# Writing the one-hot comparisons of a graph layer's edge stage as three-operand instructions

## The reference, cut to what matters

```
x_src = node_embeddings[src];  x_dst = node_embeddings[dst];  e = edge_emb[edge_type]
messages = (x_src + e) @ msg_W + msg_b
att_in = concatenate([x_src, x_dst, e, task_rep], axis=-1)
edge_delta = tanh(_gelu(att_in @ att_W1 + att_b1) @ att_W2 + att_b2)
edge_weight = 1.0 + edge_scale * edge_delta
messages = messages * edge_weight
agg = segment_sum(messages, dst, num_segments=n_nodes)
deg = segment_sum(edge_weight[:, 0], dst, num_segments=n_nodes)
```

## Time and profile before

| | us |
|---|---|
| median of 3 runs | 1439.61 |
| the three runs | 1430.62, 1439.61, 1441.83 |
| profiled execution | 1435.78 |
| its span in the trace | 1433.9 |
| POOL, DVE, PE busy in the span | 960.2, 901.2, 920.2 |

### The profile page before, as it was taken

One profiled execution on the slowest core, in us unless ns is written; L12 is line 12 of the kernel. 1 busy time (PEld: TensorE's weight loads), 2 busy tenths in 40 slices (PEclk: granted clock), 3 DMA queues, 4 the chain that ended last, 5 costly groups with the idle time before them and its releaser, 6 DMA issues. The chain is left out here.

```text
span 1433.9 us, 18420 instructions
## 1 busy us (share of the span) xinstructions
PE 920.2 (64%) x4908; PEld 710.1 (50%) x4908; DVE 901.2 (63%) x2653; ACT 614.9 (43%) x1493; POOL 960.2 (67%) x906
## 2 busy tenths in 40 slices
PE   5503232321135110488879999999899999998795
PEld 4402122221125100376767776767677777766464
DVE  5466575656566544146547887777777777876357
ACT  5424333333334333122245665555555555654334
POOL 3477777777777776485566777777777777776012
PEclk9856566665555555698999999999999999999788
DMA  5477566566856565237355777777777777778402
GB/s 149 121 194 273 194 199 220 202 207 201 304 195 215 195 215 199 53 97 181 96 167 172 217 219 216 212 208 218 215 212 217 216 218 222 216 211 176 107 16 75
DMA packets 105090, 266.56 MB, mean 186 GB/s; under 512 B 25067, under 2 KB 45680, under 8 KB 98848
## 3 DMA queue, kind: packets, MB, share of 16 engines
q0 software_dynamic: 54560, 166.61, 39.8%
q1 hardware_dynamic: 48640, 97.03, 21.3%
q10 hardware_dynamic: 1792, 1.75, 0.4%
HBM read 195.82 MB, written 68.81 MB: 185 GB/s over the span
## 5 line engine op out<-in xcount | busy, mean ns | idle before, releaser
L670 POOL DMA_INDIRECT gath<-hp_d,chain_src x391 | 387.0, 990 | 131.4 <-issue 121.0
L1333 POOL DMA_INDIRECT gbuf<-pm_d,srcs x357 | 384.1, 1076 | 123.3 <-issue 104.2
L904 DVE SCALAR_TENSOR_TENSOR hist<-hist,smask,gath 128x256 f32<-128x256 f32 x390 | 189.1, 485 | 207.6 <-ACT gath L700 199.5
L700 ACT ACTIVATE gath<-gath,chain_w 128x256 f32<-128x256 f32 x391 | 167.4, 496 | 336.6 <-DMA gath<-hp_d,chain_src 336.6
L1440 PE MATMUL ps<-qw,halves 128*128 x1275 | 212.5, 275 | 41.3 <-DMA gbuf<-pm_d,srcs 23.8
L1646 DVE TENSOR_TENSOR acc<-ps,acc 112x272 f32 x425 | 186.9, 440 | 77.1 <-DVE acc L1646 47.4
L1442 PE MATMUL ps<-gbuf,ident 128*128 128x256 f32 x714 | 214.3, 382 | 0.0
L822 PE MATMUL ps<-win_hot,node_hot 128*112 128x28 bf16 x391 | 42.3, 246 | 234.2 <-DVE win_hot L1003 234.2
L1514 ACT ACTIVATE gbuf<-ps 128x512 f32<-128x512 f32 x180 | 107.5, 598 | 193.0 <-PE ps L1442 192.7
L1440 PEld LDWEIGHTS ps<-qw,halves 128*128 128x128 bf16 x1275 | 125.1, 98 | 124.1 <-issue 59.7
L1461 PE MATMUL ps<-gbuf,placed 128*112 128x272 f32 x714 | 179.0, 393 | 1.0 <-ACT placed L1535 1.0
(11 more groups left out here) (277 smaller groups left out, 1398.9 us busy)
## 6 DMA issues: line engine op xcount, KB each, us to landing
hist_d<-hist SPq DMA_DIRECT2D x48, 1024.0 KB, 4.5
pm_d<-gbuf SPq DMA_DIRECT2D x7, 896.0 KB, 5.5
gath<-hp_d,chain_src POOLq DMA_INDIRECT x391, 3.0
wn<-node_row_d SPq DMA_DIRECT2D x27, 224.0 KB, 3.5
key<-node_row_d SPq DMA_DIRECT2D x26, 224.0 KB, 3.3
gbuf<-pm_d,srcs POOLq DMA_INDIRECT x357, 4.0
hp_d<-hpo SPq DMA_DIRECT2D x7, 448.0 KB, 3.2
hb_d<-gbuf SPq DMA_DIRECT2D x7, 448.0 KB, 3.4
```

The source lines that it names most:

```text
L670: eng.indirect_dma_start(row_at(j), None, hp_d[:, :], bass.IndirectOffsetOnAxis(ap=chain_src[:, j:j + 1], axis=0)).then_inc(got[q % RINGG] ...
L700: eng.activation(row_at(j), row_at(j), ACT.Copy, scale=chain_w[:, j:j + 1]).then_inc(gw_ready, 1)
L904: eng.scalar_tensor_tensor(out=state_at(j), in0=state_at(j - 1) if j else first_state[:, :], scalar=smask[:, j:j + 1], in1=row_at(j), op0= ...
L1333: eng.indirect_dma_start(gath3(g % RING)[:, k, 0:2 * D], None, pm_d[:, :], bass.IndirectOffsetOnAxis(ap=srcs[:, g * SG + k:g * SG + k + 1] ...
```

## The change

Three comparisons of the edge stage are written as `scalar_tensor_tensor`, which computes (in0 op0 scalar) op1 in1. `hot`: the keys are compared with `pcol` as before, and the result is multiplied by `onec`, read 512 times over. Types and places: 0.0 is added to the index, and the result is compared with the edge's number. The values written are the same. DVE waits once more, for `one_set`, ahead of the stage. No instruction is added, dropped or moved on any engine; three change their kind.

```
 def match_keys(g):
     n, at = g // KG, g % KG * GW
     eng.wait_ge(key_in[n % 2], (n // 2 + 1) * 32)
-    eng.tensor_scalar(hot[g % 2], key[n % 2][:, at:at + GW], pcol[:, 0:1], None, ALU.is_equal).then_inc(hot_ready, 1)
+    eng.scalar_tensor_tensor(out=hot[g % 2], in0=key[n % 2][:, at:at + GW], scalar=pcol[:, 0:1],
+                             in1=onec.to_broadcast([P, GW]), op0=ALU.is_equal, op1=ALU.mult).then_inc(hot_ready, 1)
+eng.wait_ge(one_set, 1)
 match_keys(0)
...
     if has(g):
         e0 = g * (2 * SG)
-        eng.tensor_tensor(gath3(r)[:, :, 2 * D:SW], bc(iof[:, 0:TY], SG), bi(edgef[:, e0:e0 + SG], TY), ALU.is_equal)
-        eng.tensor_tensor(place[r % 3][:, :].rearrange("p (k t) -> p k t", k=SG), bc(iof[:, 0:WIN], SG),
-                          bi(edgef[:, e0 + SG:e0 + 2 * SG], WIN), ALU.is_equal).then_inc(match_ready, 1)
+        eng.scalar_tensor_tensor(out=gath3(r)[:, :, 2 * D:SW], in0=bc(iof[:, 0:TY], SG), scalar=0.0,
+                                 in1=bi(edgef[:, e0:e0 + SG], TY), op0=ALU.add, op1=ALU.is_equal)
+        eng.scalar_tensor_tensor(out=place[r % 3][:, :].rearrange("p (k t) -> p k t", k=SG), in0=bc(iof[:, 0:WIN], SG),
+                                 scalar=0.0, in1=bi(edgef[:, e0 + SG:e0 + 2 * SG], WIN),
+                                 op0=ALU.add, op1=ALU.is_equal).then_inc(match_ready, 1)
```

## The result

The changed kernel took 1420.14 us, the median of 4 runs (1415.54 to 1424.87); the kernel before, run beside it on the same chip, 1435.11 us (4 runs, 1429.71 to 1441.83). The ratio is 0.9882, with a 95% interval of 0.9851 to 0.9913: 1.2% faster, 17 us by this ratio (the two medians differ by 15.0 us), where the forecast was 30 us and 1406 us. The profiled execution took 1415.54 us with a span of 1413.5 us, 20.4 us less than the profiled span before.

A forecast was written before the change was run, and what follows sets the result against it. POOL's gathers were taken to bound the edge stage at 5.47 us a group; falling to 5.16, between PE's 5.10 and VectorE's 5.23, over 97 groups saves 30 us from 1436: 1406 us, range 1393 to 1434.

The forecast's parts named there:

- GpSimd sets the pace: Edge stage: four gathers with 0.30 us ahead of each take 5.50 us, against 5.47 us a group measured.
- L1636, 0.35 us of VectorE, costs POOL half a microsecond: Edge stage, short key comparison: once a group a gather takes about 1.44 us where 0.95 is undisturbed.
- the even-spread formula: Gathers starting evenly: a VectorE instruction of length L holds them (L - 0.17)^2 / 2 / 1.25 us a group.
- end less 0.12: A gather starting inside a VectorE instruction with two SBUF inputs is released 0.12 us before that instruction's end.
- the locking: Edge stage: gathers fall in step with VectorE's 5.03 us period, the last held only 0.03 us by the new key comparison.
- I take 5.16: Edge stage's expected us a group, between PE's floor 5.10 and VectorE's 5.23; from 5.47 now, 30 us gained.
- VectorE's catching up: Edge stage: VectorE, 0.15 us over PE's 4.88 in ordinary steps, recovers in the 14 long ones, 1.4 us to spare.
- VectorE's lag doesn't reach PE: Edge stage: PE waiting for `halves` or `placed` would show VectorE's longer step reaching PE and the forecast wrong.
- the second, holds spread evenly: Edge stage: evenly spread holds, or the new instruction at its upper bound, 5.32 to 5.44 us a group; chance 0.17.
- No hold (the first): Edge stage: by the skill's rule no gather is held, 5.10 us a group, 1394 to 1400 us; chance 0.12.
- Running on into the next instruction (the third): Edge stage: the key comparison's hold continues into the first L1659, 5.49 us a group, 1438 us; chance 0.10.
- The fourth: Edge stage: places, key comparison and L1659 hold as one 1.51 us block, 5.93 us a group, 1481 us; chance 0.08.

The follow-up runs named there:

- the padded runs: The kernel before, short key comparison kept, an unused sum over 256 columns (0.41 us) put behind it; three runs: 1558.88, 1571.24, 1576.85 us, ratios 1.0017, 0.9934, 1.0017.

## Why the prediction came out right, and where it failed

- **GpSimd sets the pace: right.** The gathers' mean fell by 0.053 us, four a group over 97 groups make 21 us, and the stage became 20 us shorter. On the chips where GpSimd waits for PE instead, shorter gathers moved the time by nothing that repeated.
- **"L1636, 0.35 us of VectorE, costs POOL half a microsecond": this step failed.** The gather of the earlier trace rows is held by L1650, which starts 0.01 us before it, and with L1650 left out such a gather takes 0.94 to 0.99 us. Of 0.50 us a group, 0.33 stand at the types and places, 0.14 at the keys, 0.05 elsewhere (rounded). Even of the 0.14 only about 0.05 is L1636's own, if it lets a gather go 0.13 us before its end as in the padded runs; the other 0.09 is L1659's behind it. The half microsecond a group put on L1636 was about 0.05. The row of L1650 stood beside the gather in the very group that I cited; I took the instruction that started inside the gather, and priced L1650 at 0.08 us by the even-spread formula. What should have warned me: the same arithmetic that the prediction used for L904, end less 0.12, fits L1650 to 0.01 us and says nothing of L1636 there.
- **The gain came nevertheless, by the locking** that the prediction had as its second argument: with a step of about 5.03 us four gathers fit one step and fall into the same place each time. It named the wrong place (0.60 us into the key comparison; it is 0.03), but the period was right, 5.03 us predicted and measured. That the range held rests on this and on the measured size of the holds, 0.50 us a group, which stayed right whichever instruction made them; it was luck that writing L1636 longer removes holds of another instruction.
- **"I take 5.16": mis-sized, 5.27 measured.** The gain was 20 us in the profiled executions, not 30, and the forecast proper, 5.10 to 5.23 us a group and 1400 to 1412 us, was missed; the mean gather is 1.023 us, not 0.96 to 1.01. That VectorE's catching up would bring the stage close to PE's pace left out the holds that remain. Of them 0.14 us a group stand at the places, 0.11 at the keys and about 0.06 elsewhere. VectorE's step is 5.5 to 5.6 us at each long group of PE (6.39 us), which breaks the lock, and in most cases a gather meets the place comparison right after it; and 12 of the 63 gathers that start inside the key comparison are held by up to 0.92 us.
- **The three-operand key comparison: right,** 748 ns against 0.75; **types and places cost nothing: right,** 215 and 617 ns.
- **VectorE's lag doesn't reach PE: right.** PE's ordinary groups are 4.88 us and its long ones about 6.4, as before, and VectorE's waits for GELU fell from 40.8 + 15.8 us to 16.9 + 1.1. "Busy about 43 us more" came out as 30.4 in the page: the key comparison did add 80.0 - 37.1 = 42.9, but the custom instructions behind it became 8 us shorter; the rest I didn't trace.
- **The rivals.** The nearest in pace is the second, holds spread evenly: 5.32 us a group predicted, 5.27 measured, although the holds aren't spread evenly at all. No hold (the first) is refuted by 801.57. Running on into the next instruction (the third) happens: that gather, started 0.03 us into the key comparison, ends at 803.43, 0.95 us after 802.48, and the key comparison ended at 802.28, so it was held into the custom instruction behind it. Under the new form it happens 12 times in 101 groups. In the kernel before it was the usual course, 25 of the 31 gathers that started inside L1636, as the prediction saw at 780.45 and gave to this rival alone, not to its own account of the half microsecond. And a start within the first 0.05 us doesn't escape by itself: 24 of those 25 started 0.04 or 0.05 us into L1636. The fourth, a block from the place comparison through to the custom instruction, is refuted: gathers held by the place comparison are let go before it ends, under the long key comparison as under the short.

## What to carry to other kernels

When two engines disturb each other, look at every instruction that overlaps the one that is held, and fit the moment of release to the end of each; the one that starts in its middle is only one candidate, and a count over all gathers sorted by their start can tell them apart without a run. Where a periodic step of one engine meets a periodic queue of another, a step as long as the queue's can be worth more than a shorter one: 0.4 us of added VectorE work a group shortened the gathers, and the kernel with it became faster. And such a gain lasts only where that queue sets the pace: on another chip the same kernel gained nothing that could be told.

## What the runs showed of the hardware

- A place comparison with two SBUF inputs, 0.62 us, holds a gather that starts within its first 0.45 us, until 0.12 us before its end, and then the gather takes its full 0.95 us (1.42 to 1.46 us for a start at its beginning).
- A gather that starts 0.17 to 0.24 us before the types comparison, 0.21 us with two SBUF inputs, is caught by it (1.24 us at 903.54); with the place comparison behind, it takes up to 1.80 us (1.78 at 1196.17). Gathers 0.32 us or more ahead of the types comparison, 0.45 ahead of the places, aren't held. Why one that already runs for 0.2 us is held and starts over, no run here shows.
- The Trainium skill, "SBUF — State Buffer", "Who interferes with whom", says that an instruction with two SBUF inputs contends with what GpSimd reads, and infers that it leaves the writing of descriptors alone. For these gathers the measurement decides otherwise: 1.43 us with it, 0.94 to 0.99 without. The gathers read their row numbers from SBUF (`srcs`); whether that is the reason, no run here shows.
- The short key comparison and a gather hold each other. A gather that starts 0.03 to 0.06 us into it takes 1.10 to 1.13 us where a sum stands behind it, and up to 1.46 us with the custom instruction directly behind. A key comparison that starts 0.52 us into a gather takes 0.53 or 0.54 us in place of 0.35 in 25 of 40 cases. The same section says that in VectorE's two-port modes, which a comparison of this kind with one tensor can enter, whoever issues first blocks the other; those gathers and the 25 cases agree, the other 15, with a gather of 0.98 or 0.99 us and an undelayed comparison, don't quite. It excepts the form that also writes a sum, and the 35 gathers of 0.94 or 0.95 us agree.
- A three-operand comparison of 512 bf16 columns with a second tensor of float32 ones takes 748 ns, the same comparison of one tensor 0.35 us, and with a sum written as well 740 ns and 83 to read it.
- One program took 1436, 1556 and 1579 us on three chips of the same kind, at a mean granted clock of 0.80 to 0.81 on the first and 0.78 to 0.80 on the others. Where the difference comes from, no run here shows; in the trace of the changed kernel on the third, waits of up to 6.8 us are put down to no instruction of the kernel ("remote").
